# Attention: order of ScalarE's copies and exponentials, place of the values' projection, and an early table load

## The reference

```python
# B, S, D = 4, 256, 256;  H, G = 16, 4;  HD = D // H = 16;  KV = HD * G = 64
qkv = x @ Wqkv + bqkv
q, k, v = jnp.split(qkv, [D, D + KV], axis=-1)
q = q.reshape(b, s, H, HD)
k = jnp.tile(k.reshape(b, s, G, HD), (1, 1, H // G, 1))
v = jnp.tile(v.reshape(b, s, G, HD), (1, 1, H // G, 1))
scores = jnp.einsum('bqhd,bkhd->bhqk', q, k) / HD
prob = jax.nn.softmax(scores, axis=-1)
out = jnp.einsum('bhqk,bkhd->bqhd', prob, v).reshape(b, s, D)
return out @ Wout + bout
```

## Time and profile before

| | us |
|---|---|
| median of 3 runs | 1164.42 (1162.85 to 1165.55) |
| the profiled execution | 1165.31 |
| its span, first to last instruction | 1163.4 |
| attention in it, from the first layernorm's end to the last residual | about 16 to 161 |

### The profile page before, as it was taken

One profiled execution on the slowest core, in us unless ns is written; L12 is line 12 of the kernel. 1 busy time (PEld: TensorE's weight loads), 2 busy tenths in 40 slices (PEclk: granted clock), 3 DMA queues, 4 the chain that ended last, 5 costly groups with the idle time before them and its releaser, 6 DMA issues. The chain is left out here.

```text
span 1163.4 us, 13471 instructions
## 1 busy us (share of the span) xinstructions
PE 998.6 (86%) x3916; PEld 622.6 (54%) x3916; DVE 873.8 (75%) x1141; ACT 570.2 (49%) x1207; POOL 707.0 (61%) x507
## 2 busy tenths in 40 slices
PE   5788767999999999995949886999789887786898
PEld 2555545888888888883415432443344333232477
DVE  3667745877777787776458779978999789999862
ACT  1766642344344434432655766563755574464141
POOL 2366621556565555551358787987899789989100
PEclk9999976999999999997969997998999989899989
DMA  3000004524433342413045455554466445645001
GB/s 97 1 1 0 0 19 149 152 82 121 126 118 100 97 144 78 125 50 96 25 109 129 139 165 148 128 162 110 127 153 156 117 124 149 159 142 143 0 1 37
DMA packets 60529, 115.74 MB, mean 99 GB/s; under 512 B 11025, under 2 KB 16145, under 8 KB 60353
## 3 DMA queue, kind: packets, MB, share of 16 engines
q1 hardware_dynamic: 59344, 113.30, 35.3%
q10 hardware_dynamic: 1136, 1.90, 0.5%
HBM read 113.66 MB, written 1.51 MB: 99 GB/s over the span
## 5 line engine op out<-in xcount | busy, mean ns | idle before, releaser
L1519 POOL TENSOR_TENSOR uB<-u,rows_B 128x512 f32<-128x512 f32 x256 | 319.8, 1276 | 38.4 <-DVE da L1669 35.6
L883 POOL TENSOR_TENSOR lutw<-lutw,lt 128x865 f32<-128x865 f32 x80 | 187.3, 2341 | 161.1 <-DVE lt L860 155.4
L1687 PE MATMUL ya<-hV,ident 128*128 128x512 f32 x336 | 197.5, 675 | 74.5 <-DVE hV L1611 74.2
L1669 DVE TENSOR_TENSOR_SCAN da<-da,uB 128x512 f32<-128x512 f32 x168 | 201.2, 1220 | 36.8 <-ACT da L1598 31.8
L1687 PEld LDWEIGHTS ya<-hV,ident 128*128 128x128 f32 x336 | 63.7, 207 | 176.5 <-DVE hV L1611 136.7
L1528 POOL TENSOR_TENSOR hP<-hS,rows_C 128x512 f32<-128x512 f32 x88 | 111.9, 1272 | 36.1 <-DVE hS L1666 18.6
L1666 DVE TENSOR_TENSOR_SCAN hS<-da,uB 128x512 f32<-128x512 f32 x88 | 106.6, 1211 | 17.7 <-ACT da L1597 8.2
L1597 ACT ACTIVATE da<-zero 128x2 f32<-128x2 f32 x256 | 43.1, 168 | 150.8 <-DVE hV L1611 149.4
L1611 DVE TENSOR_TENSOR hV<-da,rows_C 128x512 f32<-128x512 f32 x168 | 112.0, 667 | 0.0
L838 ACT ACTIVATE ah<-ups 128x1024 fp32r<-128x1024 f32 x40 | 41.2, 1029 | 121.7 <-DVE ups L856 121.7
L1687 PE MATMUL ya<-hP,ident 128*128 128x512 f32 x176 | 96.0, 629 | 0.0
(11 more groups left out here) (320 smaller groups left out, 2085.9 us busy)
## 6 DMA issues: line engine op xcount, KB each, us to landing
rows_B<-bc_rows SPq DMA_DIRECT2D x128, 256.0 KB, 3.6
rows_C<-bc_rows SPq DMA_DIRECT2D x128, 256.0 KB, 4.3
wr<-in_moe_w SPq DMA_DIRECT2D x41, 384.0 KB, 4.2
cwb<-cw_rows SPq DMA_DIRECT2D x16, 512.0 KB, 4.0
cwb<-cw_rows SPq DMA_DIRECT2D x16, 384.0 KB, 4.9
cwb<-cw_rows SPq DMA_DIRECT2D x16, 256.0 KB, 3.8
lut_f<-in_lut_idx SPq DMA_DIRECT2D x1, 2160.0 KB, 9.5
cwb<-cw_rows SPq DMA_DIRECT2D x16, 128.0 KB, 5.0
```

Of the source, the lines that this page charges most:

```text
L883: e.tensor_tensor(part, part, lt[:, q, :], ALU.add).then_inc(s_la, 1)
L1519: e.tensor_tensor(uB[:, n % UBUF, :], u[:, seg % 2, d, :], RB[:, q, :], ALU.mult).then_inc(s_ub, 1)
L1669: e.tensor_tensor_scan(a[:, way], a[:, way], uB[:, n % UBUF, way], 0.0, ALU.mult, ALU.add).then_inc(s_sc, 1)
L1687: return e.matmul(ya[n % 2][:, :], g.ident[:, :], at, start=False, stop=False, skip_group_check=True).then_inc(done, 1)
```

## The change

Three edits in `attention`. "v" becomes piece 13 and is no longer piece 11, so that the second half's keys of pair 1 are piece 11 (copied by VectorE) and the first query piece is piece 12 (copied by ScalarE); the steps now pack 10 and 11, nothing, 12 and 13, 14 to 16, and 17 to 20. ScalarE loads the table set of the exponentials at the head of its program. In ScalarE's step, `second_copy` comes ahead of `exps`.

```diff
         FIRST = len(pieces) // NH
-        pieces.insert(FIRST + 1, ("v",))
+        pieces.insert(FIRST + 3, ("v",))
...
-        PER_STEP = [range(FIRST, FIRST + 3)] + [range(FIRST + 1 + 2 * i, FIRST + 3 + 2 * i) for i in range(1, 5)]
-        assert PER_STEP[-1][-1] == len(pieces) - 1
+        PER_STEP = [range(FIRST, FIRST + 2), (), range(FIRST + 2, FIRST + 4), range(FIRST + 4, FIRST + 7),
+                    range(FIRST + 7, len(pieces))]
...
+                e.preload_act_table_set("exp_and_others")
                 e.wait_ge(s_k, 1)
                 e.activation(kh[:, :], kps, ACT.Identity, bias=wt.bk[0:KV, 0:1]).then_inc(s_kh, 1)
...
                         unpack(t)
+                    if at := unit(b, i, TURN):
+                        second_copy(*at)
                     if at := unit(b, i, SCORES):
                         exps(*at)
-                    if at := unit(b, i, TURN):
-                        second_copy(*at)
                     if at := block_end(b, i, VALUES):
                         heads_out(*at)
```

## The result

| | before | after |
|---|---|---|
| median | 1163.63 us (4 runs, 1162.53 to 1165.55) | 1148.13 us (4 runs, 1145.84 to 1152.11) |
| ratio | | 0.9869, 95% interval 0.9835 to 0.9902 |
| the profiled execution, its span | 1165.31, 1163.4 | 1149.53, 1147.7 |

The account below looks back on a forecast made before the run. Bound: TensorE's turns waiting for ScalarE's copy, held by program order. Order 11.8, packing 1.8, table 0 and clock 1.3 sum to 14.9 us, giving 1150.4 or 1149.5, forecast as 1150.0 us; range 1146 to 1154.5, stretched to 1145.5 to 1156.5.

Parts of the forecast that it names:

- What bounds it: Attention loop: TensorE's turns wait 15.4 us in 8 waits for ScalarE's copy, queued behind exponentials though its input was ready.
- The order, 11.8 us: ScalarE's loop step: copy ahead of exponentials saves 11.8 us, 2.2 at the first two waits and 9.6 at six others.
- The walk: One turn of the attention loop, four units, reckoned with durations of before: 12.0 us against 13.5 from turn 12 to 16.
- The new wait: ScalarE in the loop: the copy of unit 13 delays exponentials of unit 16 by 0.6 us, but they still gain.
- The packing, 1.8 us: Start of attention: fewer pieces ahead of first scores, turn 0 earlier by 1.8 us, from 1.3 to 2.1.
- The table, 0 with the packing moved: First exponentials: early load of 1.28 us would be hidden anyway with the packing moved, worth 0 to 0.3, counted 0.
- The clock, 1.3 us: Loop at 77.2 to 80 us: half clock vanishes with TensorE's long idle times, 1.3 us, between 0 and 1.3.
- Rival (b): Stages behind the attention: earlier work meets the clock differently, 3 us either way, 1147 to 1153; chance 0.77 with the forecast.
- (a): Attention loop gives half, 6 us, as turns wait for GpSimd's normalisation: 8.4 us in all, 1156.0; chance 0.13.
- (c): ScalarE's exponentials wait behind late copies at all 16 odd units; at 1.1 us each the kernel takes 1167.1; chance 0.04.
- (d): Compiler still puts a table load ahead of first exponentials, costing nothing, or one in the loop, 1154; chance 0.04.
- The bounds that I listed for the range: Whole kernel: start 1.3 to 2.1, clock 0 to 1.3, loop 10.5 to 13, later clock 3 us either way.

Follow-up runs that it names:

- the order alone: Kernel before with one edit only, ScalarE's second copy ahead of its exponentials: 1152.12 us, ratio 0.9892.
- packing alone: Kernel before with only the moved packing, table load still in front of the first exponentials: 1164.96 us, ratio 1.0002.
- the kernel before with the added operation: Kernel before plus one VectorE operation at the head of the layernorm behind the attention: 1163.88 us, ratio 0.9994.
- the runs with one copy each: Kernel after, but with copies ahead of exponentials only for units 3 mod 4: 1154.60 us; only for units 1 mod 4: 1161.91 us.
- table: Kernel before with only the early table load: 1163.74 us, ratio 0.9997.
- packing with the added operation: Kernel before with the moved packing, plus one VectorE operation at the head of the layernorm behind the attention: 1162.64 us, ratio 0.9985.
- the half copies: Kernel after, with ScalarE copying one of the two banks of every unit rather than of odd units alone: 1145.93 us, ratio 0.9841.
- with the heads' copy ahead: Kernel with ScalarE copying one bank of every unit, plus ScalarE's copy of heads ahead of the exponentials of its step: 1142.70 us, ratio 0.9816.
- with the projection: The kernel with the heads' copy ahead, plus TensorE's block projection ahead of the values' product of the same step: 1140.44 us, ratio 0.9783.
- with the residual: The kernel with the projection ahead, plus VectorE's residual addition at the head of its step: 1139.38 us, ratio 0.9786.

## Why the prediction was right

- *What bounds it.* The wait of TensorE for ScalarE's copy was one of order: the row fell from 15.4 us to none with the order alone.
- *The order, 11.8 us.* Measured 11.0: T to R without half clocks was 107.8 before (109.03 less the 1.24 of its one half clock; packing alone gives the same, 110.14 less two) and 96.80 after. The walk gave 12.0 us for the turn of the loop; it measured 12.1. By turns of unit: from 0 to 8 it gave 3.57 (2.2 and 1.6 were reckoned), from 8 to 12 2.64, of which 1.24 are the clock's, from 12 to 28 6.23 (1.56 for each four units), and the last steps took 0.2 more than before. The term is 0.8 too high, spread over all of them. The half clock's 1.24 is taken against the next turn of the loop; the same turn, 8 to 12, took 13.66 in the kernel before with the added operation, at a granted clock of 1.00, by which the half clock cost 1.10 and the order gave 11.1.
- *The new wait.* The walk had the copy of odd units 1 mod 4 hold exponentials by 0.6 us with no effect, and the copy of units 3 mod 4 in idle time. Both are in the rows at 92.59 and 97.92, and the runs with one copy each put nearly all of the gain on the second kind.
- *The packing, 1.8 us.* Measured 2.22 to 2.24, a bit over my upper bound of 2.1. Scores 0 came 15.47 us after K, 15.55 were walked (38.6 less 23.05). I took 0.3 off for the values' copy on GpSimd, which didn't cost.
- *The table, 0 with the packing moved.* Shown by the whole change without it (25.60 against 25.58). Alone it is worth 1.43.
- *The clock, 1.3 us.* No half clock in the loop after, as forecast. Between turns 8 and 28 one or two came in 4 of the 6 executions that kept the holes of 2 us (before, packing, table, packing with the added operation), and in none of the 8 without them. So the holes seem to be needed there and don't suffice, from one execution each. At 49 to 55 us there was one in the order alone and one in the kernel before with the added operation, behind an idle time of TensorE of 2.5 us ahead of scores at about 48 us, which the kernel before has too, without a half clock. The price was right for this execution, that a half clock lay in it was luck in part, and the reason is open.
- *Rival (b)*, the clock elsewhere, is the one that is alive beside the forecast. The four times of after spread over 6 us, which it would fit, though only one of the four has a profile. In the profiled executions a second half clock in the loop took 1.1 us of the packing's gain and 1.2 us of the table load's. I had it at 3 us either way; the one scan segment alone moved by up to 3.4 us. That R to the end came out equal was luck: up to the segment after had gained 2.8 us on before, in it it lost 1.8, and behind it 1.1.
- *Rivals (a), (c), (d).* The loop gave its whole gain, not half; ScalarE's wait for turns is 6 us outside of the last steps, and the kernel without the copies of units 1 mod 4 ahead has no shorter loop; one load was put, in the place that the change gives it.

The forecast of 1150.0 us stands beside 1148.13. The profiled execution came to 15.7 us less in span, where I had 14.9; 1.4 of it lie ahead of K and are the clock's, which I hadn't forecast, so the parts that I had reckoned gave 14.4 (2.2 and 12.2), 0.5 under my sum. The mechanism held; that the total lies as near is luck in part. The bounds that I listed for the range add up to 1145.0 to 1155.6 and not to 1146 to 1154.5; the measured time lies in either.

## What to carry to other kernels

Where an engine waits for another's short operation, look at what stands ahead of that operation in the other's own program and whether its input was ready: a copy of 0.6 us behind exponentials of 1.8 us cost 11 us here, and moving it needed no faster engine. After such a move look at the next short operation with the same fault, since the half copies gave 2.0 us from T to R, with the heads' copy ahead 6.5, with the projection 8.5 and with the residual 10.3. They were measured only in this order of adding; what the heads' copy gives by itself isn't known. And judge a part of 1 to 2 us by a stretch of the trace between fixed points, not by the kernel's time, when the granted clock of later stages moves by as much.

## What the hardware showed beyond expectation

- A segment of unchanged instructions took 119.7 to 120.0, 121.3 or 123.0 to 123.1 us in 14 executions, and executions that entered it within 0.06 us of each other differed by 1.6 us. An added operation of 1.23 us on the path ahead of it left the kernel at 0.9994 of its time (0.9985 to 1.0003).
- The eight matmuls of the keys' projection took 5.3 us in all in one execution (after) and 6.6 in another (before), the same instructions after the same idle time of 2.2 us, which moved K by 1.4 us. In a third (half copies with the heads ahead) they took 3.6 us.
